# GRU recurrence in the order r, n, z: which gate's product TensorE forms second, and which accumulators VectorE turns first

## What is computed

```python
def cell(h, x):
    gi = x @ W_ih + b_ih
    gh = h @ W_hh + b_hh
    i_r, i_z, i_n = jnp.split(gi, 3, axis=-1)
    h_r, h_z, h_n = jnp.split(gh, 3, axis=-1)
    r = jax.nn.sigmoid(i_r + h_r)
    z = jax.nn.sigmoid(i_z + h_z)
    n = jnp.tanh(i_n + r * h_n)
    h_new = (1.0 - z) * n + z * h
    return (h_new, h_new)
```

## Time and profile before

| what | us |
| --- | --- |
| median of 3 runs | 2704.85 |
| lowest and highest | 2703.67, 2705.14 |
| the profiled execution | 2705.32 |
| its span, first to last instruction | 2703.5 |
| PE busy, whole span | 2537.0 (94%) |
| DVE busy | 1943.2 (72%) |
| POOL busy | 1228.1 (45%) |
| ACT busy | 1078.8 (40%) |

### The profile page before, as it was taken

One profiled execution on the slowest core, in us unless ns is written; L12 is line 12 of the kernel. 1 busy time (PEld: TensorE's weight loads), 2 busy tenths in 40 slices (PEclk: granted clock), 3 DMA queues, 4 the chain that ended last, 5 costly groups with the idle time before them and its releaser, 6 DMA issues.

```text
span 2703.5 us, 159498 instructions
## 1 busy us (share of the span) xinstructions
PE 2537.0 (94%) x69506; PEld 1991.7 (74%) x69506; DVE 1943.2 (72%) x7034; ACT 1078.8 (40%) x3639; POOL 1228.1 (45%) x3026
## 2 busy tenths in 40 slices
PE   5688797878999999999999999999999999999999
PEld 2334343537888788888888888888888888888888
DVE  3767677665666877777787778777777777878622
ACT  5374727263333333333333333333333333333333
POOL 1535333133332555455545545554554555455454
PEclk9799999899999999999999999999999999999999
DMA  4100000001111333233333323333332333333254
GB/s 170 56 3 18 3 17 3 2 2 43 49 51 51 94 97 96 84 105 94 92 99 94 92 86 107 92 100 93 92 99 86 99 96 94 91 87 90 84 152 134
DMA packets 144747, 209.40 MB, mean 77 GB/s; under 512 B 16432, under 2 KB 86320, under 8 KB 143664
## 3 DMA queue, kind: packets, MB, share of 16 engines
q1 hardware_dynamic: 142896, 195.01, 24.0%
q10 hardware_dynamic: 1152, 4.19, 0.4%
HBM read 185.51 MB, written 13.63 MB: 74 GB/s over the span
## 4 chain that ended last, share of the span: by engine, by line
PE 71%; DVE 3%; POOL 1%; issue 1%; ACT 1%; DMA 0%; DVEq 0%; POOLq 0%; ACTq 0%
PE ps L1216 27%; PE ps L1251 25%; PE ps L1266 12%; PE ps L1228 6%; PE ps L1240 2%; POOL hidf L908 1%; DVE turn_n L1097 0%; DVE fresh L1110 0%; DVE turn L1100 0%; DVE hcur L1115 0%; DVE hcur L1112 0%; DVE npre L1103 0%; ACT cand L1004 0%; POOL hid L920 0%; DVE h L1113 0%
## 5 line engine op out<-in xcount | busy, mean ns | idle before, releaser
L1216 PE MATMUL ps<-whh,hcur 128*32 128x128 f16 x49152 | 792.2, 220 | 24.0 <-DVE hcur L1115 12.0
L1216 PEld LDWEIGHTS ps<-whh,hcur 128*32 128x32 f16 x49152 | 694.5, 97 | 147.4 <-DVE hcur L1115 119.3
L1251 PE MATMUL ps<-hb,w 128*128 128x256 f16 x6400 | 781.8, 273 | 0.1
L1251 PEld LDWEIGHTS ps<-hb,w 128*128 128x128 bf16 x6400 | 602.9, 98 | 95.4 <-DMA w<-in_w 0.4
L900 POOL COPY hb<-hcur 128x32 f16<-128x32 f16 x512 | 169.6, 331 | 665.3 <-DVE hcur L1115 665.3
L997 ACT ACTIVATE r<-ur 128x16 f32<-128x16 f32 x512 | 110.6, 216 | 826.6 <-DVE ur L1091 826.6
L1266 PE MATMUL ps<-hid,w 128*128 128x256 f16 x3200 | 428.3, 273 | 2.2 <-POOL hid L920 1.8
L1266 PEld LDWEIGHTS ps<-hid,w 128*128 128x128 bf16 x3200 | 312.3, 98 | 39.8 <-issue 3.0
L908 POOL TENSOR_TENSOR hidf<-up 128x256 f32<-128x256 f32 x400 | 291.8, 729 | 97.8 <-POOL hid L920 51.0
L920 POOL TENSOR_TENSOR hid<-hidf,hid 128x256 f16<-128x256 f32 x400 | 269.0, 672 | 62.2 <-ACT hid L993 62.2
L1088 DVE STREAM_TRANSPOSE turn<-ps 128x128 f32<-128x128 f32 x512 | 161.8, 316 | 179.5 <-PE ps L1216 170.4
(11 more groups left out here) (155 smaller groups left out, 3222.5 us busy)
## 6 DMA issues: line engine op xcount, KB each, us to landing
w<-in_w SPq DMA_DIRECT2D x400, 256.0 KB, 2.7
w<-in_w SPq DMA_DIRECT2D x400, 128.0 KB, 2.7
gi_scratch<-gis SPq DMA_DIRECT2D x72, 128.0 KB, 1.7
spare<-gi_scratch SPq DMA_DIRECT2D x36, 128.0 KB, 2.8
gi<-gi_scratch SPq DMA_DIRECT2D x36, 128.0 KB, 2.7
x2T<-in_xT SPq DMA_DIRECT2D x4, 1024.0 KB, 7.1
out<-xo ACTq DMA_DIRECT2D x8, 512.0 KB, 4.3
stage<-in_W_hh SPq DMA_DIRECT2D x1, 3072.0 KB, 10.8
```

The source lines that it names most:

```text
L1216: mm = pe.matmul(ps[j * COLS:(j + 1) * COLS, bank, 0:P], hcur[:, k], whh[:, s, k, at:at + P], start=(k + s == 0), stop=(k == KT - 1 and s ...
L1251: mm = pe.matmul(ps[:, UB[u], w * TOK:(w + 1) * TOK], w13[:, u, w, k], hb[:, f % 2, s, k].rearrange("p b t -> p (b t)"), start=(w + k + s ...
```

## The change

TensorE forms the products of a step in the order r, n, z instead of r, z, n; the weights, the banks and the semaphores of each gate stay as they were. On VectorE the transposition of z's accumulators moves from the end of `early` to `late`, behind the transposition of n's. No instruction is added or removed. GpSimd's and ScalarE's streams stay as they were.

```diff
@@ -1089,12 +1089,12 @@
                 dve.wait_ge(r_turned, g + 1)
                 dve.wait_ge(gates_set, g + 1)
                 nc.vector.tensor_reduce(ur[:], parts_of(turn[:, u, 0]), AX.X, ALU.add).then_inc(ur_ready, 1)
-                dve.wait_ge(z_done, g + 1)
-                nc.vector.transpose(turn[:, u, 1, :, 0:COLS], ps[:, ZB, 0:P].rearrange("p (k c) -> p k c", c=COLS)).then_inc(z_turned, 1)
 
             def late(g, u):
                 dve.wait_ge(n_done, g + 1)
                 nc.vector.transpose(turn_n[:, :, 0:COLS], ps[:, NB, 0:P].rearrange("p (k c) -> p k c", c=COLS)).then_inc(n_turned, 1)
+                dve.wait_ge(z_done, g + 1)
+                nc.vector.transpose(turn[:, u, 1, :, 0:COLS], ps[:, ZB, 0:P].rearrange("p (k c) -> p k c", c=COLS)).then_inc(z_turned, 1)
                 dve.wait_ge(n_turned, g + 1)
                 dve.wait_ge(r_ready, g + 1)
                 nc.vector.tensor_tensor(parts_of(turn[:, u, 2])[:, :, :, 0:3], parts_of(turn_n[:])[:, :, :, 0:3],
@@ -1208,7 +1208,7 @@
         def _(pe):
             def scan_step(g):
                 pe.wait_ge(h_ready, g + 1)
-                for gate, (bank, done) in enumerate(((RB, r_done), (ZB, z_done), (NB, n_done))):
+                for gate, bank, done in ((0, RB, r_done), (2, NB, n_done), (1, ZB, z_done)):
                     for k in range(KT):
                         for s in range(2):
                             for j in range(P // COLS):
```

## The result

The changed kernel takes 2748.29 us (median of 4, 2747.6 to 2750.95) against 2704.41 for the kernel before; the ratio is 1.0164, 95% interval 1.0149 to 1.0179. That is 44 us slower, where 47 were forecast, and inside the range. The profiled execution took 2747.72, its span is 2745.3, 41.8 more than before.

A forecast was written before the change was run, and what follows sets the result against it. Blocks 1 to 7 were taken as bound by TensorE's queue, only just ahead of the state loop; step terms of 16.6, 25.4, about 1, 1.2 and about 3 us give 47 over 2704.85, so 2752 us, range 2738 to 2768.

The forecast's parts named there:

- The loop: The way through the state from one recurrent step to the next: grows by 0.21 us, from 3.62 to 3.83.
- The n side: The multiplication by r and npre come 0 to 0.12 us earlier, a gain lost because cand waits behind omz.
- The cover: TensorE's own queue hides part of the longer loop: a step lasts as long as the longer of the two.
- The 81 short ones: Steps of blocks 1 to 7 below 3.70 us, at the loop's limit: 0.205 us each, 16.6 us slower.
- the 299: Steps of blocks 1 to 7 between 3.70 and 3.80 us, mean 3.745: 0.085 us each, 25.4 us slower.
- the late chunks: Steps in which the expert chunk's work on VectorE makes r's transposition late: about 3 us slower.
- block 0: Its 52 steps of 3.97 us cover the longer loop; its 12 short ones give 1.2 us.
- The 67 longer steps: Steps of blocks 1 to 7 with mean 3.97 us, mostly covered by their own matmuls: about 1 us slower.
- A: GpSimd's zs held until VectorE's multiplication ends: loop 0.09 us longer, 37 us more, 2789 us; chance 6%.
- B: Faster: ScalarE has z and omz done before npre, loop 3.50 us, 9 us less, 2696 us; chance 3%.
- C: Some of the z side's links shorten when late: loop grows by only 0.14 us, 2729 us; chance 5%.
- D: TensorE's gap of 0.21 us is a wait for the state, no step has slack: 107 us, 2812; chance 2%.

The follow-up runs named there:

- e1: The kernel before with only TensorE's order changed to r, n, z, VectorE's order as before; 2745.43 us, ratio 1.0156.
- e4: The changed kernel with GpSimd's two additions for z replaced by one VectorE sum behind the multiplication by r; 2692.6 us, ratio 0.9960; run again, 2690.96 us.
- e7: The changed kernel without the second of the two matmuls of each down product; 2729.96 us, ratio 1.0114 against the kernel before.
- e5: The kernel before, order r, z, n kept, with GpSimd's two additions for z replaced by one sum on VectorE; 2703.64 us, ratio 1.0011.
- e2: The kernel before with only VectorE's order changed, n's transposition ahead of z's, TensorE still r, z, n; 2834.76 us, ratio 1.0485.
- e3: The changed kernel with ScalarE's tanh put ahead of z's two sigmoids; 2735.66 us, ratio 1.0119 against the kernel before.
- e6: The kernel before without the second of the two matmuls of each down product; 2650.15 us, ratio 0.9813.

## Why the prediction was right, point by point

**The loop.** Forecast: z's transposition moves by 0.36, `cand` from 2.55 to 2.76 from the step's start, the loop from 3.62 to 3.83. Measured: 0.36, 2.76, 3.82. The links over GpSimd and ScalarE kept their lengths to 0.01. The 0.01 that is missing sits behind `cand`: where `cand` runs right behind `omz`, it lasts 0.20 and `fresh` follows it by 0.33, not by 0.35 as in the earlier trace rows. Over some 440 steps that is about 5 us less.

**The n side.** Forecast: the multiplication starts up to 0.12 earlier, and that is lost. Measured: at 1.82 instead of 1.93, and `npre` waits 0.45 for ScalarE.

**The cover.** By classes of the old step length, in blocks 1 to 7, I compared each step with the same step after. The 81 short ones grew by 16.6 us (forecast 16.6), the 299 with lengths from 3.70 to 3.80 by 28.1 (forecast 25.4 and 3 for the late chunks), block 0 by 1.9 (forecast 1.2). These are the steps of the sum that held in size.

That the 299 came out so close is partly luck. The loop is 0.01 shorter than forecast, and something that the forecast doesn't have made up for it. In 14 steps of blocks 1 to 7, the same ones in both kernels and often 22 apart, one of VectorE's last state instructions starts late though what it waits for is there, so that `fresh` starts 0.57 to 0.68 behind `cand` in place of 0.33. One of them, before and after:

```profile
1292.84 0.18 DVE L1106 TENSOR_TENSOR zh<-z,h 128x16 f32<-128x16 f32 x1
1293.33 0.17 DVE L1110 TENSOR_TENSOR fresh<-cand,omz 128x16 f32<-128x16 f32 x1 [0.31 <-ACT cand L1004]
```

```profile
1303.68 0.18 DVE L1106 TENSOR_TENSOR zh<-z,h 128x16 f32<-128x16 f32 x1 [0.54 <-ACT omz L1000]
1304.17 0.17 DVE L1110 TENSOR_TENSOR fresh<-cand,omz 128x16 f32<-128x16 f32 x1 [0.31 <-DVE zh L1106]
```

`fresh` starts 0.49 behind `zh` in both rows, where 0.24 is usual after the change. Before, `zh` was early and most of that was hidden; after, it is on the way. These steps grew from 3.80 to 4.13 on average, 4.5 us in all, of which the forecast's rule accounts for about one. Why VectorE is late there is open.

**The 67 longer steps are the term of the sum that failed.** I had written that they are "mostly covered by their own matmuls, about 1 us". They got shorter, by 5.0 us in all, from a mean of 3.97 to 3.89. All but two of them have 18 or 20 expert matmuls like the others. They were long because TensorE had stopped or slowed in the middle of its recurrent product: the product's weight loads take 1.35 in a usual step, and over 1.38 in 60 of the 67. In the kernel before, a stop, and a step in which the product takes 1.53 with no single gap long enough for the profile to list:

```profile
1152.80 0.68 PEld L1216 LDWEIGHTS ps<-whh,hcur 128*32 128x32 f16 x47 [0.21 <-DVE hcur L1115]
1154.53 0.73 PEld L1216 LDWEIGHTS ps<-whh,hcur 128*32 128x32 f16 x49 [1.06 <-issue]
...
2132.00 1.53 PEld L1216 LDWEIGHTS ps<-whh,hcur 128*32 128x32 f16 x96 [0.21 <-DVE hcur L1115]
```

The waits of the weight loads in blocks 1 to 7, before:

```profile
PEld ps L1216 <- DVE hcur L1115: 112.0, 445, 1.2
PEld ps L1216 <- issue: 11.7, 34, 1.1
```

and after:

```profile
PEld ps L1216 <- DVE hcur L1115: 163.5, 448, 1.4
PEld ps L1216 <- issue: 3.9, 11, 0.8
```

The listed stops fell from 11.7 to 3.9 us. With the smaller ones, the products of the 67 steps took about 16 us more than 1.35 each before, and about 3 after. A step count by length can't tell a full queue from a queue that stood still; the length of the recurrent product and the number of matmuls in the row would have. With 16.6 + 28.1 + 1.9 - 5.0 the classes give 41.6 of the 41.8 that the spans are apart. The term of the longer steps, +1 in the forecast and -5 in the trace, is 6 us and so the whole distance to 47; the other misses are under 1 us each. The 299 stand at 3.839 on average after the change, where the undisturbed loop is 3.82: 9 of the 14 steps above are among them (2.6 us), 24 with a late chunk (1.2 us) and 4 with a stop (1.5 us).

**The rivals.** A (GpSimd held by VectorE): `zs` took 0.22 in every step and started at its usual 0.39 to 0.40 behind the transposition in nearly every one. The test was weak, since the multiplication turned out to last 0.20 and `zs` starts 0.04 before its end. e1 tests it better: there `uz` starts 0.15 into a multiplication of 0.24, and it too takes its usual 0.22 and starts its usual 0.30 behind `zs`. B (faster): e4 shows that its mechanism exists once z's way is 0.30 shorter: 9 us were given to it at a loop of 3.50, and e4's kernel is 10 to 11 us below the kernel before, at a loop of 3.51. C (a loop of 3.76) is out by the measured 3.82, D (no cover) by the 44 us themselves and by e7. That TensorE's late z is the cause is shown by e1, and that it works over the length of z's way by e4, with e5 against the thought that GpSimd's relief alone is the gain.

## What to carry to other kernels

In a recurrence ask of each gate how long its way is behind the product, and give the last place on TensorE to the gate with the shortest way; here z's (two additions on GpSimd, two sigmoids, and the tanh in ScalarE's queue behind them) was longer than n's, though n's looks like the heart of the cell. The change of order paid here only together with the change that shortens the way of what comes last. And where one engine's queue and a loop are nearly the same length, count the steps at each limit: a gain is capped at the steps where the loop leads, a loss is not.

## What the runs showed of the hardware

An instruction's duration in the trace depended on what stood ahead of it. The multiplication L1100 lasted 0.24 right behind the transposition that it waits for (e1 and e5), and 0.20 behind a transposition that it doesn't need (after and e2). It lasted 0.28 to 0.29 in some 360 of the 512 steps of the kernel before, where `uz` had started on GpSimd 0.02 to 0.04 ahead of it. A GpSimd addition that had started longer ahead cost nothing: in e1 `zs` starts 0.15 ahead and is still running, and the multiplication takes 0.24. In those 360 steps GpSimd's copy L893 also starts inside the multiplication, and no run separates the two. A tanh right behind the sigmoids lasted 0.20, one that followed a wait 0.22.

TensorE stopped in the middle of the recurrent product, where it waits for nothing, and by and large the more, the shorter the steps: 1.4 us in e2 (4.03 a step on average in blocks 1 to 7), 3.7 to 4.7 after and in e1, e3 and e7 (3.82 to 3.85), 9.4 in e5 and 11.7 before (3.75 and 3.76), 10.2 and 7.5 in the two runs of e4's kernel (3.73), 21.7 in e6 (3.68). I compared the stops with the packets of the queue that carries instructions (in the kernel before 407 packets of 16 KB in that stretch, about one each 4.1 us). In the kernel before 26 of 32 stops begin 2.05 to 2.65 us after a packet's start, where chance alone would put 5. Where they end is sharper: all 227 stops of the ten traces end 2.15 to 3.00 us after a packet's start, where chance would put about a fifth of them. The Trainium skill, page "Runtime: NRT & Kernel Launch", section "Instruction fetch mechanics", says that an engine's instructions are refilled in blocks of 16 KiB and that the cost of crossing one is "mostly hidden". The 16 KB packets agree with the first, and here some 11 us of 1680 were not hidden. That the stops are late refills is argued from this coincidence and was not tried by an experiment of its own.
